# Linear attention's last chunk: three of the six gate and up pairs of the chunk in front moved behind its contexts

## The reference, cut to what matters

```python
x = x + _L0_attn_ref(_layernorm(x), Wq, bq, Wk, bk, Wv, bv, gamma, beta)   # linear attention
x = x + _L0_ffn_ref(_layernorm(x), w_gate, w_up, w_down)                  # gated feed-forward, 768 hidden
...
# linear attention, 32 sequences of 64 rows, 16 heads of 16
q, k = relu(x @ Wq.T + bq), relu(x @ Wk.T + bk);  v = x @ Wv.T + bv
kv = einsum('bnhd,bnhp->bhdp', k, v);  k_sum = k.sum(axis=1)
out = einsum('bnhd,bhdp->bnhp', q, kv) / maximum(einsum('bnhd,bhd->bnh', q, k_sum), 1e-6)
y = out + x;  return layernorm(y) * gamma + beta
# feed-forward
h = silu(x @ wg.T) * (x @ wu.T);  return h @ wd.T
```

## Time and profile before

| what | us |
|---|---|
| median of 3 runs | 1988.75 (1988.57 to 1992.19) |
| profiled execution, its own time | 1987.96 |
| its span | 1986.2 |
| PE busy | 1941.3 (98%) |
| DVE, ACT, POOL busy | 1232.3, 1112.4, 600.2 |

### The profile page before, as it was taken

The page is one execution under the profiler, slowest core; times in us unless marked ns, Lnnn a source line. Parts: engine busy times, 40 slices in busy tenths (PEclk is TensorE's granted clock), DMA queues, the critical chain, the costliest instruction groups (busy, mean ns, idle before and its releaser), DMA issues.

```text
span 1986.2 us, 43991 instructions
## 1 busy us (share of the span) xinstructions
PE 1941.3 (98%) x17307; PEld 1694.8 (85%) x17307; DVE 1232.3 (62%) x3579; ACT 1112.4 (56%) x2432; POOL 600.2 (30%) x652
## 2 busy tenths in 40 slices
PE   6999999999999998998999999999999999999998
PEld 6898998989898984777688887889999999999998
DVE  7767777776767666776688988438758623243212
ACT  5666666666666663333577877544444444444443
POOL 3111141112211101233122211444444444444444
PEclk9999999999999999999999999999999999999999
DMA  5656454455445431000311011001010010101000
GB/s 202 185 174 205 148 166 151 151 174 151 158 152 166 144 123 48 1 1 1 92 43 37 25 33 40 6 1 64 1 43 22 22 43 1 43 1 43 1 12 32
DMA packets 100332, 154.21 MB, mean 78 GB/s; under 512 B 12896, under 2 KB 78752, under 8 KB 100000
## 3 DMA queue, kind: packets, MB, share of 16 engines
q1 hardware_dynamic: 100128, 151.41, 24.3%
HBM read 103.73 MB, written 43.45 MB: 74 GB/s over the span
## 4 chain that ended last, share of the span: by engine, by line
PE 46%; ACT 2%; DVE 2%; issue 1%; POOL 0%; POOLq 0%; DVEq 0%; ACTq 0%
PE bank L83 21%; PE bank L1132 18%; PE bank L1053 2%; PE bank L1068 1%; PE bank L1040 1%; ACT att_p L1238 1%; PE bank L1098 1%; PE bank L1009 1%; ACT att_pt L1243 1%; PE bank L1079 0%; DVE dec_room L140 0%; POOL right_h L963 0%; ACT att_kt L1230 0%; PE bank L1091 0%; DVE att_vz L1385 0%
## 5 line engine op out<-in xcount | busy, mean ns | idle before, releaser
L963 POOL TENSOR_TENSOR right_h<-right_hr,right_h 128x512 fp32r<-128x512 f32 x256 | 340.9, 1332 | 418.3 <-ACT right_hr L1285 418.3
L1284 ACT ACTIVATE right_h<-bank,dec_b 128x512 fp32r<-128x512 f32 x256 | 176.3, 689 | 389.6 <-PE bank L83 365.0
L83 PE MATMUL bank<-lat_kv_t,lat_qk 128*128 128x320 f32 x1536 | 253.7, 314 | 2.8 <-DVE lat_qk L2456 2.8
L83 PE MATMUL bank<-lat_wv,lat_kv_t 128*128 128x512 f32 x960 | 242.1, 393 | 0.0
L83 PEld LDWEIGHTS bank<-lat_kv_t,lat_qk 128*128 128x128 f32 x1536 | 227.6, 188 | 15.5 <-DVE lat_qk L2456 6.4
L2320 ACT ACTIVATE lat_p<-bank,lat_neg_max 128x320 f32<-128x320 f32 x256 | 134.6, 527 | 148.4 <-DVE lat_neg_max L2461 148.4
L83 PEld LDWEIGHTS bank<-lat_wv,lat_kv_t 128*128 128x128 f32 x960 | 175.1, 188 | 30.4 <-DVE lat_qk L2456 0.4
L83 PE MATMUL bank<-dec_xt,dec_lo 128*128 128x512 f32 x512 | 200.7, 392 | 0.0
L2461 DVE TENSOR_REDUCE lat_neg_max<-bank 128x1 f32<-128x320 f32 x256 | 122.5, 486 | 93.6 <-PE bank L83 87.6
L1285 ACT ACTIVATE right_hr<-bank,dec_b 128x512 f32<-128x512 f32 x256 | 174.4, 681 | 0.0
L1132 PE MATMUL bank<-dec_hi,right_h 128*128 128x256 f32 x1024 | 161.6, 280 | 1.2 <-POOL right_h L963 1.2
(11 more groups left out here) (332 smaller groups left out, 3806.6 us busy)
## 6 DMA issues: line engine op xcount, KB each, us to landing
lat_turns<-lat_pb SPq DMA_DIRECT2D x63, 640.0 KB, 3.0
lat_pt<-lat_turns SPq DMA_DIRECT2D x252, 160.0 KB, 3.2
raw_w<-in_L_ffn_W SPq DMA_DIRECT2D x16, 1024.0 KB, 6.6
lat_ctx_raw<-in_ctx SPq DMA_DIRECT2D x16, 512.0 KB, 5.3
right_ctx_raw<-in_ctx_turned SPq DMA_DIRECT2D x16, 512.0 KB, 3.7
lat_kv_f<-in_ctx_turned SPq DMA_DIRECT2D x15, 512.0 KB, 4.3
lat_ctx_raw<-gate_rows SPq DMA_DIRECT2D x15, 512.0 KB, 4.8
lat_kv_t<-lat_lt SPq DMA_DIRECT2D x32, 128.0 KB, 4.4
```

What stands on the lines that cost most here:

```text
L83: mm = pe.matmul(out, lhs(a, k), rhs(b, k), start=first and k == 0 and n == 0, stop=last and k == KD - 1 and n == 2)
L963: pool.tensor_tensor(h[:, g % 2, 1, :], hr[:, g % 2, :], h[:, g % 2, 0, :].bitcast(F32), ALU.subtract).then_inc(h_lo, 1)
L1284: act.activation(h[:, n % 2, 0, :], h_bank[n % 2][:, :], ACT.Relu, bias=bias).then_inc(h_hi, 1)
```

## The change

In the last chunk alone, pairs (2,3), (2,4) and (2,5) come after the contexts of tile 15; slots 3 and 4 of the chunk have no pair. `IN_SLOTS = NH - 3` is 3. Chunks 1 and 2 stay as they were. The number of instructions is the same; the order changes on PE, ACT, DVE and POOL:

```diff
# POOL, last chunk
+            for h in range(IN_SLOTS):
+                hidden_low(last - 1, h)
+            near.norm.power(pool, last - 2)
+            norm_y.power(pool, last)
+            hidden_low(last - 1, IN_SLOTS)
+            hidden_low(last - 1, IN_SLOTS + 1)
+            shift_of_ffn(last)
+            hidden_low(last - 1, IN_SLOTS + 2)
# PE
                 for i in range(PER + 1):
-                    if c >= 1:
+                    if c == NCH - 1:
+                        if i < IN_SLOTS:
+                            gate_up(c - 1, i)
+                    elif c >= 1:
                         gate_up(c - 1, i)
...
-                if c >= 1:
+                if c == NCH - 1:
+                    for h in range(IN_SLOTS, NH):
+                        gate_up(c - 1, h)
+                elif c >= 1:
                     gate_up(c - 1, NH - 1)
# ACT
-                    if c >= 1:
+                    if c >= 1 and (c < NCH - 1 or i < IN_SLOTS):
                         gate(c - 1, i)
                         high(c - 1, i)
...
-                    gate(c - 1, NH - 1)
-                    high(c - 1, NH - 1)
+                    for h in range(IN_SLOTS if c == NCH - 1 else NH - 1, NH):
+                        gate(c - 1, h)
+                        high(c - 1, h)
# DVE
+                    between(i)          # in scale_rows, ahead of slot i's work
...
-                    if c >= 1:
+                    if c >= 1 and (c < NCH - 1 or i < IN_SLOTS):
                         hidden(c - 1, i)
...
-                if c >= 1:
-                    hidden(c - 1, NH - 1)
-                scale_rows(c)
+                if c == NCH - 1:
+                    hidden(c - 1, IN_SLOTS)
+                    scale_rows(c, lambda i: hidden(c - 1, IN_SLOTS + 1) if i == 3 else None)
+                    hidden(c - 1, IN_SLOTS + 2)
+                else:
+                    if c >= 1:
+                        hidden(c - 1, NH - 1)
+                    scale_rows(c)
```

More of the change, by code:

```diff
@@ L206, in linear_feed @@
     PER = NT // NCH
+    IN_SLOTS = NH - 3
     with ExitStack() as ctx:
@@ L303, in _ @@
             shift_of_ffn(0)
-            for c in range(1, NCH):
+            for c in range(1, NCH - 1):
                 add_beta(c)
@@ L315, in _ @@
                 shift_of_ffn(c)
+            last = NCH - 1
+            add_beta(last)
+            for h in range(IN_SLOTS):
[6 more added lines that the diff above has]
+            hidden_low(last - 1, IN_SLOTS + 2)
             for h in range(NH):
@@ L611, in y_row, with scale_rows @@
                 norm_y.row(dve, y[:, t % PER, :], t)
-            def scale_rows(c):
+            def scale_rows(c, between=lambda i: None):
                 dve.wait_ge(norm_y.rstd_ready, c + 1)
```

## The result

The changed kernel takes 1992.6 us, median of 22 runs (1991.36 to 1995.53), against 1988.83 of the kernel before (22 runs, 1987.68 to 1992.19): ratio 1.0019, 95% interval 1.0013 to 1.0025. It is slower by 3.8 us. The forecast of 1988.8 was wrong, and the measured time lies outside its range. What happened is rival A, at more than its price.

What follows compares the result with a forecast made beforehand. PE was taken as the bound, busy 1941.3 of 1986.2 us, with 6.6 us lost around two holes. Terms -2.16 + 0.29 + 3.30 - 1.41 = 0.0 gave a median of 1988.8 us, range 1986.2 to 1991.4.

Steps and rivals of the forecast that it cites:

- rival A: Clock falls near 904 behind the new hole; pair (2,3) at half rate delays DVE's chain: +1.5, 1990.3 us; chance 0.22.
- step 2: Up to the scaling: y statistics close 2.16 us earlier, at 907.26; product of (2,3) just ready; scaling begins at 908.37.
- the sum: Last chunk: -2.16 statistics, +0.29 stalls and product, +3.30 close to release of `down(2,2)`, -1.41 clock, together 0.0 us.
- Step 1: Up to the last contexts: PE's new hole about 3.2 us, contexts of 15 at 903.59, pair (2,3) 6.6 us later.
- Just in time: Product of (2,3) can start at 907.22, 3.01 us after its pair's first matmul, with DVE ready at 907.26.
- Steps 3 and 4: Scaling and after: POOL stretches second scaling and last add, ffn statistics close 916.15, low part of (2,5) done 918.84.
- Step 5: PE's end of chunk: `down(2,2)` released at 919.84, +1.43; its 18 matmuls at full clock, -1.41; `turn_ffn` at 922.19.
- the signs that the prediction named: Hole about 3 us, y statistics 2.2 earlier, stretched scaling and add, low-part wait 1.2, full clock 918 to 922, pair 925.2.
- Its decision point: The clock rival decides once pair (2,3) starts later than 904.25, the product being due within 0.04 us of DVE's readiness.

Runs made afterwards that it cites:

- e1: The changed kernel plus three unused matmuls in PE's hole ahead of the contexts of tile 15; 1989.18 us, ratio 1.0003 to the kernel before.
- e9: The changed kernel plus one unused matmul in PE's hole ahead of the contexts of tile 15; 1988.93 us, ratio 0.9998 to the kernel before.
- e2: The changed kernel with the near statistics of chunk 1 moved between the pairs of chunk 3, no filler; 1988.85 us, ratio 1.0000 to the kernel before.
- e7: The kernel before with POOL's low part of (2,4) ahead of the y power in the last chunk; 1989.80 us, ratio 1.0004.
- e6: The kernel before with POOL's low part of (2,4) early, near statistics later and two unused matmuls ahead of `down(2,2)`; 1988.02 us, ratio 0.9997.

## Why the prediction was wrong, step by step

The step that failed is step 2: it took the clock behind the new hole at full, and the sum had no term for its fall. e1 is the changed kernel with the clock held, so it tests the queue arithmetic alone. Its times, put back by 1.40 so that the contexts of tile 13 start where they did before, and the changed kernel's, put back by 1.01:

| step | forecast | e1 | changed |
|---|---|---|---|
| 1: contexts of 15 start on PE | 903.59 | 903.40 | 903.40 |
| 2: product of (2,3) starts | 907.26 | 907.16 | 909.96 |
| 3: product of (2,4) starts | 911.68 | 911.64 | 913.92 |
| 4: product of (2,5) starts, behind the close | 916.16 | 916.18 | 918.46 |
| 5: `down(2,2)` starts | 919.84 | 920.05 | 922.33 |
| first pair of chunk 3 | 925.21 | 925.33 | 927.61 |

- *Step 1* was right: a hole of 2.97 us, forecast 3.2. Its consequence for the clock stood in no term of the sum.
- *Step 2* is the step that failed. "Just in time" held at full clock only (e1: within 0.1 us). With pair (2,3) at half clock its product came 2.7 us late, and `scale_rows` stood behind it on DVE. About 0.5 of this was made up later, where the scaling no longer waits for POOL's power; 2.3 is left at the first pair (927.61 against 925.33).
- *Steps 3 and 4* were right with the clock held, to 0.04 us. In e1 POOL's low parts stretched the second scaling and the last add, as computed. In the changed kernel, everything being later, the low part hit the third scaling instead (1.52), and the last add again (1.26). The low part of (2,5) was late next, as said: PE waited 1.31 for it, forecast 1.2.
- *Step 5* was right on the clock in the first trace, 2.26 from `down(2,2)` to the turning, and wrong in the second, where the clock fell here as well. Of the signs that the prediction named, PE's wait for the low part and the clock of 1.00 in 918 to 922 are in the first trace; the first pair of chunk 3 is later than 927.
- *Rival A* named place and mechanism, with 0.22. Its price was mis-sized: 1.5. A whole pair at half rate, as its text has it, takes 2.75 longer (16.51 / 6); a delay of 1.5 fits a half clock of about 3.4 us, the length of the fall in the trace before (918.6 to 922.0). It was 6.8 us, and +2.4. Its decision point, a start of the pair later than 904.25, was met at 905.52 - 1.01 = 904.51, because the contexts ahead of it were slow already; in e1 it is 904.02.
- *Its chance* was too low because I compared hole with hole, 3.2 against 3.50, and argued that PE had done nothing at all ahead of the old fall. e9 and e2 show falls behind holes of 1.91 and 1.66 us with small matmuls around them.
- *The range* ended at 1991.4, 1.1 above A at its price of 1.5, so A at 2.4 and a further fall had no room in it. The terms of the sum did cancel, as forecast: e1 has D at 30.4, against 30.3 before. What decided was the clock near 904, which the sum left at its favourable value.

## What to carry to other kernels

A pair that stands between two waits of PE can also be what keeps PE's clock up. Before moving it, count the new hole, then price the half clock behind it not at one length but at the lengths that falls have been seen to take (here 3.4 and 6.8 us), on the instruction that comes next on the engine that waits for PE. Where dense matmuls follow a hole of 2 to 3 us, filling it with unused matmuls is worth a trial; here it returned the whole 2.3 us, but the two of e6 left 2.50 us of a larger hole and the clock fell. To let DVE scale ahead of the product that waits for PE would be another way; it was not tried. And a POOL pass that collides with DVE gains nothing by a move to another place on the same chain (e7, e6).

## What the runs showed of the hardware that I had not expected

The clock fell near holes of 1.66, 1.91, 2.50 and 2.97 us (0.4, 1.4 and 1.2 us behind the first three, inside the last) and stayed at half for 3.4 us, at the last for 6.8, while PE was already fully busy again for most of that time. The length of the hole does not set that of the fall: 3.50 us brought 3.4 in the kernel before, 4.22 brought 6.8 in e7. The Trainium skill, page "TensorE: Matmul & The Clock Gate", section "HAM oscillation — how this bites in real kernels", warns of idle gaps of PE from a certain length on, and all four of these holes are shorter than that. By that rule alone none of them should have brought a fall; the granted clock and the matmuls' own durations above say otherwise, and they decide. The holes here lie beside small matmuls and other short waits, which may be the difference; no run here separates that. Falls near 754 us come and go between runs of the same kernel. And a hole of 2.97 us in both traces of the changed kernel brought the same 6.8 us: I can't say whether that is so in every run, since only the mean clock is known for the others, and two of them have it as high as most runs of the kernel before (0.998).
